# Two transformer layers on one core: another hand-over order for the five engines, the same steps

## The reference

```
xn = layernorm(x)
x = x + attn0(xn) + ffn0(xn)
xn = layernorm(x)
x = x + attn1(xn) + ffn1(xn)
```

## Time and profile before

| | |
|---|---|
| median of 3 runs | 600.06 us (599.37 to 602.33) |
| the profiled execution: its span | 601.7 us |
| its own time, from the first to the last instruction | the same 601.7 us, the last store's landing within it |
| TensorE busy | 562.0 us (93%) |
| ScalarE busy | 469.6 us (78%) |
| VectorE busy | 426.6 us (71%) |
| GpSimd busy | 233.6 us (39%) |
| granted clock of TensorE, mean | 0.983 |
| DMA | 30.40 MB, mean 51 GB/s |

### The profile page before, as it was taken

The page is one execution under the profiler, slowest core; times in us unless marked ns, Lnnn a source line. Parts: engine busy times, 40 slices in busy tenths (PEclk is TensorE's granted clock), DMA queues, the critical chain, the costliest instruction groups (busy, mean ns, idle before and its releaser), DMA issues. The chain is left out here.

```text
span 601.7 us, 13300 instructions
## 1 busy us (share of the span) xinstructions
PE 562.0 (93%) x5153; PEld 290.7 (48%) x5153; DVE 426.6 (71%) x909; ACT 469.6 (78%) x607; POOL 233.6 (39%) x302
## 2 busy tenths in 40 slices
PE   3687898999999999999999999999999999999976
PEld 1332434433555555645544555565445454456654
DVE  5658889988789558856699877565555365658765
ACT  2378899999988997999878898777979877972631
POOL 3748666043533163306855641360232150250100
PEclk9778999999999999999999999999999999999989
DMA  8810101102041223030110330531301304035632
GB/s 265 303 36 2 36 1 35 36 2 49 6 62 33 33 59 39 27 37 3 19 17 2 64 54 27 89 55 27 54 10 36 45 20 69 17 68 85 94 57 48
DMA packets 150914, 30.40 MB, mean 51 GB/s; under 512 B 133952, under 2 KB 149568, under 8 KB 150848
## 3 DMA queue, kind: packets, MB, share of 16 engines
q1 hardware_dynamic: 150272, 29.19, 24.4%
q10 hardware_dynamic: 576, 0.33, 0.3%
HBM read 19.02 MB, written 10.49 MB: 49 GB/s over the span
## 5 line engine op out<-in xcount | busy, mean ns | idle before, releaser
L958 ACT ACTIVATE Pt<-psS 128x1024 f32<-128x1024 f32 x288 | 281.7, 1047 | 44.8 <-PE psS L685 25.9
L699 PE MATMUL psV<-Pt,vaug 128*32 128x512 f32 x1152 | 150.3, 611 | 0.3 <-POOL Pt L1645 0.3
L1645 POOL TENSOR_SCALAR_AFFINE_SELECT Pt<-Pt 128x1024 f32<-128x1024 f32 x64 | 71.7, 1145 | 43.8 <-ACT Pt L958 43.8
L685 PE MATMUL psS<-qTf,kTf 32*128 32x512 f16 x576 | 74.9, 390 | 7.3 <-ACT Pt L958 3.7
L685 PEld LDWEIGHTS psS<-qTf,kTf 32*128 32x128 f16 x576 | 20.3, 91 | 82.9 <-ACT Pt L958 48.1
L1695 POOL TENSOR_TENSOR ss<-ss,mhalf 128x1 f32<-128x1 f32 x16 | 9.5, 596 | 111.3 <-DVE ss L1476 111.3
L699 PEld LDWEIGHTS psV<-Pt,vaug 128*32 128x32 f32 x1152 | 25.7, 109 | 41.9 <-issue 35.9
L1016 ACT ACTIVATE stage<-psS 128x1024 f32<-128x1024 f32 x32 | 31.0, 1020 | 8.1 <-PE psS L821 7.9
L1686 POOL TENSOR_TENSOR r<-qk,cos 128x256 f32<-128x256 f32 x16 | 11.9, 744 | 63.9 <-ACT qk L991 58.0
L866 PE MATMUL psB<-wguT,xhs 128*128 128x512 bf16 x108 | 27.8, 380 | 0.0
L1032 ACT ACTIVATE qtmp<-qtmp 128x1024 bf16<-128x1024 f32 x16 | 16.9, 1059 | 12.9 <-PE psA L876 8.4
(11 more groups left out here) (381 smaller groups left out, 1246.5 us busy)
## 6 DMA issues: line engine op xcount, KB each, us to landing
qkvscr<-rqkv SPq DMA_DIRECT2D x16, 384.0 KB, 2.5
G<-qkvscr SPq DMA_DIRECT2D x24, 128.0 KB, 3.7
stage<-in_wg SPq DMA_DIRECT2D x4, 512.0 KB, 8.8
w8g<-qkvscr SPq DMA_DIRECT2D x16, 128.0 KB, 3.8
oscr<-o SPq DMA_DIRECT2D x16, 128.0 KB, 3.3
at<-oscr SPq DMA_DIRECT2D x16, 128.0 KB, 2.0
out<-yout SPq DMA_DIRECT2D x16, 128.0 KB, 2.5
x<-in_x SPq DMA_DIRECT2D x1, 1536.0 KB, 12.2
```

The lines of the kernel that those rows point to most:

```text
L685: e.matmul(psS[j], kd[32 * j:32 * j + k, h, 128 * at:128 * at + 128], qd[32 * j:32 * j + k, 4 * h:4 * h + 4, :].rearrange("p s n -> p (s n ...
L699: ins = e.matmul(psV[32 * j:32 * j + 32, :], vaug[:, at, j, 32 * h:32 * h + 32], Pt[(4 * Q + j) % NP], start=(kb == 0 and h == 0), stop=(k ...
L958: e.activation(flat(Pt4[:, u % NP:u % NP + 2, :]), flat(psS4[:, j:j + 2, :]), ACT.Exp, scale=scale).then_inc(S["exp"], 1)
L1645: e.affine_select(out=p, in_=p, pattern=[[0, 8], [1, 128]], compare_op=ALU.is_ge, fill=0.0, base=0, channel_multiplier=-1).then_inc(S["mas ...
```

## The change

The five lists of ORDER are replaced. They hold the same steps as before: 791 on TensorE, 421 on ScalarE, 692 on VectorE, 146 on GpSimd, 88 on SP. No function, no wait and no buffer is changed; which of the three shared banks a step gets follows from the new list by the same rule. The lists are long; the diff below shows their heads, their ends and the lines that the prediction speaks of.

```diff
 ORDER = {
     "pe": (
-        "xnT.0 qkv.0 ts.0 xnT.1 xnT.2 qkv.1 ts.1 qxT.0 qxT.1 qk.0 xnT.3 qk.1 qkv.2 up.0 up.1 up.2 qxT.2 pv.0 qxT.3 "
-        "up.3 qk.2 pv.1 qk.3 pv.2 qk.4 pv.3 qk.5 obT.0 pv.4 qkv.3 qxT.4 qxT.5 qk.6 pv.5 td.0 xnT.4 qk.7 pv.6 up.4 "
-        "td.1 up.5 qk.8 tr.0 pv.7 attT.0 qk.9 pv.8 obT.1 qk.10 pv.9 up.6 up.7 qk.11 down.0 tr.1 xnT.5 attT.1 qkv.4 "
...
-        "qxT.8 xnT.6 up.11 pv.14 qk.16 pv.15 wo0.1 qk.17 pv.16 up.12 td.2 pv.17 qk.18 td.3 qkv.6 qk.19 tr.2 qxT.9 "
...
-        "gu.59 gu.60 PV1.13 at1T.12 gT.28 o1T.13 gT.29 hxT.26 hxT.27 dn1.12 S1.14 wo1.12 gu.61 PV1.14 at1T.13 gT.30 "
-        "gT.31 o1T.14 gu.62 S1.15 gu.63 wo1.13 PV1.15 o1T.15 hxT.28 hxT.29 dn1.13 at1T.14 wo1.14 dn1.14 at1T.15 "
-        "flagT.0 hxT.30 hxT.31 wo1.15 dn1.15"),
+        "xnT.0 qkv.0 ts.0 xnT.1 ts.1 qkv.1 qxT.0 qxT.1 up.0 qk.0 xnT.2 up.1 up.2 qkv.2 qk.1 xnT.3 qxT.2 up.3 qxT.3 pv.0 "
+        "qk.2 qkv.3 pv.1 qk.3 pv.2 qk.4 pv.3 td.0 qk.5 qxT.4 td.1 qxT.5 tr.0 pv.4 qk.6 pv.5 qk.7 up.4 up.5 up.6 qk.8 "
+        "obT.0 pv.6 up.7 obT.1 tr.1 pv.7 qk.9 pv.8 qxT.6 qxT.7 qk.10 up.8 pv.9 qk.11 xnT.4 up.9 qkv.4 down.0 qk.12 "
...
+        "pv.143 o1T.11 gu.53 xn1T.14 gu.54 obT.15 S1.12 qkv1.28 attT.15 gu.55 wo0.15 at1T.11 gu.56 PV1.12 wo1.11 "
...
+        "at1T.12 gT.28 o1T.13 wo1.12 gT.29 hxT.26 hxT.27 dn1.12 S1.14 gT.30 gT.31 gu.61 gu.62 PV1.14 S1.15 at1T.13 "
+        "o1T.14 gu.63 wo1.13 PV1.15 dn1.13 o1T.15 hxT.28 hxT.29 at1T.14 wo1.14 dn1.14 hxT.30 hxT.31 at1T.15 wo1.15 "
+        "dn1.15 flagT.0"),
     "act": (
-        "tc.0 qh.0 exp.0 exp.1 qh.1 g.0 fh.0 g.1 sq.0 fh.1 exp.2 sq.1 exp.3 exp.4 exp.5 qh.2 sin.0 exp.6 th.0 tde.0 "
...
-        "exp.19 fh.6 wh.0 g.7 tc.2 th.6 sq.7 exp.20 exp.21 th.7 fh.7 exp.22 g.8 fh.8 sq.8 tde.4 tde.5 g.9 fh.9 "
...
+        "tc.0 qh.0 wh.0 g.0 exp.0 qh.1 g.1 fh.0 sq.0 exp.1 sq.1 fh.1 exp.2 th.0 sin.0 exp.3 qh.2 exp.4 tde.0 exp.5 "
...
     "dve": (
-        "idc.0 ln0.0 vz.0 xn.0 ln0.1 ln0.2 xnTc.0 xn.1 ln0.3 xn.2 qkvc.0 xnTc.1 xn.3 tsc.0 w8.0 xnTc.2 w8.1 va.0 "
-        "q0.0 wide.0 qkvc.1 kl.0 tsc.1 kTc.0 qTc.0 w8.2 va.1 tm.0 xnTc.3 w8.3 q0.1 wide.1 qkvc.2 kl.1 w8.4 kTc.1 "
...
-        "xn1.15 gTq.13 yo.11 xn1Tc.15 yout.11 hTc.24 o1.12 hTc.25 ssm.13 osum.12 v1c.15 ro1.15 hx.13 hh.28 sg.29 "
-        "ro2.15 hh.29 sg.30 o1r.13 at1Tc.12 gTq.14 o1.13 ssm.14 hTc.26 hTc.27 osum.13 yo.12 yout.12 hx.14 hh.30 "
-        "o1r.14 at1Tc.13 gTq.15 o1.14 rng.0 osum.14 sg.31 hh.31 o1r.15 yo.13 o1.15 osum.15 ssm.15 hTc.28 hTc.29 "
-        "at1Tc.14 yout.13 hx.15 rngb.0 yo.14 yout.14 at1Tc.15 fl.0 hTc.30 hTc.31 yo.15 yout.15"),
+        "ln0.0 vz.0 xn.0 xnTc.0 ln0.1 idc.0 ln0.2 xn.1 w8.0 qkvc.0 w8.1 ln0.3 xnTc.1 xn.2 tsc.0 va.0 tsc.1 w8.2 q0.0 "
+        "kl.0 wide.0 qkvc.1 w8.3 kTc.0 qTc.0 va.1 wide.1 xn.3 xnTc.2 q0.1 qkvc.2 kl.1 xnTc.3 ge1.0 kTc.1 qTc.1 tab.0 "
+        "tm.0 ob.0 va.2 tcs.0 q0.2 ge1.1 wide.2 kl.2 qkvc.3 ln0.4 kTc.2 qTc.2 tw.0 wl.0 ge3.0 ob.1 ge3.1 ln0.5 att.0 "
...
+        "yo.11 ro2.14 v1c.14 xn1Tc.15 yout.11 hTc.24 o1.12 hTc.25 v1c.15 ssm.13 gTq.13 ro1.15 ro2.15 hx.13 hh.28 sg.29 "
...
+        "ssm.15 hTc.29 yo.14 hx.15 yout.14 hTc.30 at1Tc.15 hTc.31 rng.0 yo.15 yout.15 rngb.0 fl.0"),
     "pool": (
-        "zero.0 rs0.0 rs0.1 rs0.2 rs0.3 rope.0 ql.0 rope.1 mask.0 ql.1 mask.1 rope.2 mask.4 ql.2 mask.5 rs0.4 rs0.5 "
-        "rope.3 gz.0 rs0.6 ql.3 mask.10 mask.11 rope.4 ql.4 xf.0 rope.5 xf.1 rs1.0 rs0.7 ql.5 rs1.1 mask.18 mask.19 "
...
+        "gz.0 zero.0 rs0.0 rs0.1 rs0.2 rope.0 rs0.3 ql.0 rope.1 mask.0 ql.1 mask.1 rope.2 ql.2 mask.4 mask.5 rope.3 "
...
     "sp": (
-        "wt.2 wg.2 wg.3 wg.4 wg.5 wt.3 wt.4 wt.5 vw.0 vr.0 vw.1 vr.1 ow.0 at1r.0 vw.2 vr.2 vw.3 ow.1 at1r.1 out.0 "
...
-        "at1r.12 vw.15 out.11 ow.13 vr.15 at1r.13 ow.14 out.12 at1r.14 ow.15 at1r.15 out.13 out.14 out.15"),
+        "wg.2 wg.3 wg.4 wg.5 wt.2 wt.3 wt.4 wt.5 vw.0 vr.0 vw.1 vr.1 ow.0 at1r.0 vw.2 vr.2 vw.3 ow.1 vr.3 at1r.1 out.0 "
...
+        "ow.10 at1r.10 vr.11 vw.12 out.8 vr.12 vw.13 out.9 ow.11 at1r.11 vr.13 vw.14 ow.12 vr.14 vw.15 at1r.12 vr.15 "
+        "out.10 ow.13 out.11 at1r.13 out.12 ow.14 at1r.14 ow.15 at1r.15 out.13 out.14 out.15"),
...
```

## The result

The changed kernel takes 581.61 us (median of 4 runs, 581.26 to 582.76) against 599.73 us for the kernel before on the same chip: ratio 0.9702, 95% interval 0.9672 to 0.9731, so 17.9 us less. The forecast was 598.7 us with 592.5 at the low end. The profiled execution spans 579.5 us, against 601.7 us.

What follows compares the result with a forecast made beforehand. TensorE was taken to bound the kernel from 150 to 540 us, ScalarE as well from 60 to 150. Terms +0.3 - 1.4 + 2.3 + 0 - 3.0 = -1.8 us, 0.4 given back: -1.4, so 598.7 us, range 592.5 to 605.0.

Steps and rivals of the forecast that it cites:

- term (4): Middle: which score blocks come too early for exp changes everywhere; taken as 0, ends -4 and +4 us.
- Term (1): Start of the attention: exp.2 2.6 us late, 2.3 us of ScalarE work already done; net +0.3 us, ends -1.3 to +6.5.
- the slower rival: Opening: first score block waits for weights, exp.2 past 42 us; +6.5 instead of +0.3, 604.9 us; slower case 0.23.
- Term (2): First tiles: casts of a lose their meeting with GpSimd's gz.0; -1.4 us, ends 0 and -8, nothing counted in the middle.
- The first rival: First 150 us: all overruns from VectorE-GpSimd meetings vanish, -6 instead of -1.4, middle 1 us; 593.1 us; faster case 0.37.
- Term (3): TensorE from qk.34 on: more changes between kinds of matmul, 0.13 or 0.11 us each; +2.3 us, ends +1.5 to +4.
- Term (5): Tail: ro2.15 and vr.15 start earlier, a TensorE wait is filled, 1 us charged at the end; -3.0 us, ends -4.5 and +1.
- 0.37 for faster: Whole kernel: chance of a time below the no-change case of 597.1 to 603.1 us, through more from meetings or tail.

Runs made afterwards that it cites:

- pull_gaps: Kernel before, TensorE's list alone edited: at 28 score blocks split inside, the next step is pulled ahead of the block; 609.58 us, ratio 1.0141.
- early_qk: Changed kernel, TensorE's list alone edited: 49 score blocks are each moved ahead of the step before; 610.34 us, ratio 1.0160 to the changed kernel.
- head_new: Kernel before with the new order for everything started before 144 us, the old relative order from there on; 601.95 us, ratio 1.0008.
- tail_new: Kernel before with the old order until 519 us, the new one behind it; 597.38 us, ratio 0.9928.

## Why the prediction was wrong

**The step that failed is term (4), waits for exp in the middle, taken as 0 with ends of -4 and +4.** It measured 16.5 us in the profiled pair from exp.34 to exp.143, 14.9 without the steps that lie elsewhere now, and 12.2 us of it in the score blocks. The ends came from "the idle time to win is 4.0 us, and as much again could lie in stretched blocks", while the first part of the text had said that a stretched block counts as busy, beside 48.1 us of waits for exp in 85 waits. That total was no guide in itself: it is 43.9 us in 72 waits after the change, since most of it are loads that wait beside matmuls still running. What would have bounded the term is page part 5: the score blocks cover 74.9 us, and 144 blocks in one piece, 0.40 us as in the row of 271.20 us, come to 57.6 us, so 17 us are time beyond that, booked as busy; or, step by step in the timeline, 44 of 110 blocks show x2 and x2 where the rest have x4. The cut of the exps shows the size that was to be had in the old order without any cure by list: 385.3 to 374.1 us, 11 us. Of the other 5 us (374.1 to 368.7, both with short exps) the score blocks still hold 2.4 (39.6 against 37.2 us to the next step's load), 1.6 are the three steps that lie elsewhere now, and for the rest the runs name no cause. PV1 alone takes 2.4 us less in the new order (14.1 to 11.6), but pv, which often stands right ahead of it, takes 2.7 us more; together they have 115.4 and 115.7 us, so they hold nothing of it.

"I see no side to it" was wrong too. I found the side only afterwards, but it can be read from two lists before any run: for each pair of neighbouring score blocks, add what TensorE has to do between them and what ScalarE has to do between the two exps, at the durations of the rows. In the old order the larger of the two sums to 382.8 us over the 109 intervals, in the new one to 370.2 us; the chip took 385.6 and 369.5 us from qk.34 to qk.143. The sums match here, but their level hangs on the durations that are put in: with the medians of TensorE's steps in the two traces both come out 15 us higher, with the lower quartiles 8 us lower. Their difference of 12.6 us stays (11.8 and 12.4). And they gave pull_gaps only 4 us over before where 9.5 came in the same stretch, and for early_qk 7 of 29 us: good for the two orders, no law for edits of them.

**Term (1), the start, +0.3 us: right in the number, not in its parts.** head_new has +0.5 us (-0.7 to +1.7). The wg.2 load moved ahead took 9.41 us to landing, 14.02 to 23.43 us, as the row of the other load in that place had said (9.4); qk.0 came at 27.30 us (28.5 forecast), and exp.2 was not late at all:

```profile
23.43 0.69 DVE L1101 CAST w8g<-stage 128x1024 fp8e4<-128x1024 f32 x1 [5.40 <-DMA stage<-in_wg]
...
27.30 0.61 PE L682 MATMUL psS<-qTf,kTf 32*128 32x512 f16 x4
...
35.57 1.94 ACT L955 ACTIVATE Pt<-psS 128x1024 f32<-128x1024 f32 x2 [0.29 <-PE psS L682]
```

exp.2 was at 35.55 us before. ScalarE had done wh.0 in its idle time, as forecast. Of the two parts, 2.6 us late and 2.3 us of work in hand, the first didn't come, and head_new shows no gain from the second; that they cancelled in the forecast as well was luck. So the slower rival (604.9 us, exp.2 past 42 us) didn't come; its place was the right one to look at, its price was not paid.

**Term (2), the meetings, -1.4 us with an end of -8.** Until 144 us nothing was gained (head_new), though the longest cast did lose its neighbour. In the middle, where I counted nothing, VectorE's and GpSimd's work is worth up to 6.4 us of the gap, meetings and late results together, and what VectorE loses to the cut work of GpSimd differs by 1.6 us between the orders. "What hides its overruns is TensorE's own work" holds for the new order, which gains 2.0 and 2.5 us by the two cuts of the table, and not for the old one, which gained 5.4 and 8.9 us. The first rival, meetings at -6 and 593.1 us, had a size like this, in another stretch. Its reason, VectorE's 78.2 of 90 us ahead of 150 us, was wrong.

**Term (3), changes between kinds of matmul, +2.3 us.** No run measures it by itself. If it was paid, it is inside a middle that got 16.5 us shorter; TensorE does 328 changes from qk.34 to qk.143 where it did 308. The 0.13 us for one of them is borne out: in that stretch pv behind another kind takes 1.00 us to the next step's load, and two in a row 0.46 + 1.40 = 1.86 us, so the second saves 0.14. That the whole term is paid remains an estimate, and it decided nothing.

**Term (5), the tail, -3.0 us with an end of -4.5: right, at 4.3 us (2.6 to 6.1) for tail_new.** gT.30 starts 38.7 us behind exp.143 (43.0 before). The flag's end cost less than the 1 us charged: the span ends 3.9 us after the start of yout.15, 3.7 us before. But rng.0, which I put beside dn1.15, ends at 575.19 us, so yo.15 ends at 575.51 and yout.15 starts at 575.60 us:

```profile
573.46 1.91 PE L882 MATMUL psC<-wpT,stmp 128*128 128x256 bf16 x16
...
575.03 0.16 DVE L1525 TENSOR_SCALAR hl<-hl 128x2 f32<-128x2 f32 x1
575.09 0.42 DVE L1500 TENSOR_TENSOR yo<-psB,x 128x256 f32<-128x256 f32 x1
575.60 0.42 DVE L1509 TENSOR_TENSOR yout<-psC,yo 128x256 f32<-128x256 f32 x1
```

dn1.15's matmuls end at 575.37 us, so it was about even.

**The chances.** 0.37 for faster stood on the meetings and the tail; the mechanism that came had no case of its own among the rivals, and the range ended 11 us above the result for that.

## What to carry to other kernels

A busy TensorE is not always a working one: where banks come free in pieces, a matmul group that waits inside itself counts as busy for most of the wait, so take a line's busy time against count times one block in one piece and look for x2 and x2 in the timeline. Before costing a new order, add per score block what each of the two coupled engines has to do between its two hand-overs; the sum of the larger ones told these two orders apart, and said little of small edits. To learn what an order waits for, cut one engine's work in both orders and watch the gap; and expect little from repairing single places in a tuned order: all eight such edits and mixtures here (from 1 to 5 lists, the seams in time apart) lost 1.4 to 75%.

## What the runs showed that was not expected

The new order's middle takes 368.8 us and stays within 0.2 us of it while VectorE's work falls from 425.9 to 316.8 us, GpSimd's from 233.1 to 140.6 us or the exps from 279.4 to 169.9 us. ScalarE was busy 327.42 of the 370 us from 150 to 520 us and yet its exps cost nothing. And the price of a misplaced step is far from local: 49 score blocks moved by one step each cost 29 us, 0.6 us for each, nearly twice the 0.33 us of an unhindered block.
